# Normalised features split into rounded part and remainder before their transposition instead of after it

## The reference

```python
h = jnp.maximum(_layernorm(x), 0.0); x = x + chebyshev(h, adj)     # 4 orders, weights (4, 64, 64)
h = jnp.maximum(_layernorm(x), 0.0); x = x + attention(h, adj)     # encoder 64->128, 2 layers, 3-layer MLP
h = jnp.maximum(_layernorm(x), 0.0); x = x + gcn(h, adj)
h = jnp.maximum(_layernorm(x), 0.0); x = x + step_layer(h, adj)    # t = adj @ h; 1 where t > 0.5
```

## Time and profile before

| | |
|---|---|
| time, median of 3 runs | 767.3 us (766.12 to 768.61) |
| profiled execution, own time | 764.17 us |
| its span, first to last instruction | 762.3 us |
| busy: PE / DVE / ACT / POOL | 714.2 / 587.6 / 441.8 / 337.7 us |
| granted TensorE clock, mean share of full | 0.991 |
| L881 (split behind the transposition) | 32 x 0.69 us |
| L867 (duplicating copy) | 32 x 0.29 us (median) |

### The profile page before, as it was taken

One profiled execution on the slowest core, in us unless ns is written; L12 is line 12 of the kernel. 1 busy time (PEld: TensorE's weight loads), 2 busy tenths in 40 slices (PEclk: granted clock), 3 DMA queues, 4 the chain that ended last, 5 costly groups with the idle time before them and its releaser, 6 DMA issues.

```text
span 762.3 us, 11361 instructions
## 1 busy us (share of the span) xinstructions
PE 714.2 (94%) x3615; PEld 510.0 (67%) x3615; DVE 587.6 (77%) x1719; ACT 441.8 (58%) x933; POOL 337.7 (44%) x457
## 2 busy tenths in 40 slices
PE   8787999999999999999999999999999999989886
PEld 5365767667676767667676767767676767665663
DVE  3565688889797988889797988889797888676533
ACT  3264658564756757574756757574765747627430
POOL 4343427263553726364553726364453815422301
PEclk9999999999999999999999999999999999999999
DMA  6100100302012030202012030302012030100000
GB/s 180 63 1 0 63 15 1 88 10 84 15 33 66 8 91 1 84 15 84 14 31 68 8 91 0 84 15 84 14 26 73 8 91 6 30 1 21 1 8 7
DMA packets 37386, 30.14 MB, mean 40 GB/s; under 512 B 24016, under 2 KB 25552, under 8 KB 37328
## 3 DMA queue, kind: packets, MB, share of 16 engines
q1 hardware_dynamic: 36336, 29.20, 13.9%
q10 hardware_dynamic: 992, 0.23, 0.1%
HBM read 27.27 MB, written 2.15 MB: 39 GB/s over the span
## 4 chain that ended last, share of the span: by engine, by line
PE 70%; ACT 14%; DVE 8%; issue 4%; POOL 3%; POOLq 0%; DVEq 0%; ACTq 0%
PE turn_ps L1319 13%; PE pre_ps L1162 9%; PE post_ps L1162 7%; PE turn_ps L1285 4%; ACT negz L768 3%; PE score_ps L1270 3%; PE score_ps L1267 3%; PE score_ps L1271 3%; ACT pt L775 3%; PE qkv_ps L1249 3%; PE pre_ps L1121 3%; PE pre_ps L1178 2%; ACT z_t L789 2%; PE post_ps L1328 2%; PE pre_ps L1150 2%
## 5 line engine op out<-in xcount | busy, mean ns | idle before, releaser
L1319 PE MATMUL turn_ps<-pt,v_n 128*128 128x512 f32 x224 | 102.2, 599 | 11.0 <-ACT pt L775 11.0
L768 ACT ACTIVATE negz<-negz,negmax 128x512 f32<-128x512 f32 x128 | 91.7, 718 | 26.9 <-DVE negmax L977 26.6
L969 DVE TENSOR_TENSOR score_ps<-score_ps,a_nat 128x512 f32<-128x512 f32 x128 | 88.9, 695 | 7.9 <-PE score_ps L1271 7.3
L977 DVE CUSTOM_DVE_ANT_0 negz<-score_ps,gate 128x512 f32<-128x512 f32 x128 | 88.5, 691 | 4.5 <-POOL gate L637 0.2
L1162 PE MATMUL pre_ps<-at_hi,u_pair_pre 128*128 128x512 f32 x192 | 85.9, 447 | 4.7 <-DVE u_pair_pre L887 4.1
L566 POOL TENSOR_TENSOR rstd_post<-vareps_post,nhalf 128x4 f32<-128x4 f32 x32 | 32.7, 1020 | 115.0 <-DVE vareps_post L849 114.0
L716 ACT ACTIVATE y_t_pre<-pre_ps 128x512 f32<-128x512 f32 x48 | 28.5, 593 | 93.2 <-PE pre_ps L1162 91.8
L775 ACT ACTIVATE pt<-turn_ps 128x512 f32<-128x512 f32 x128 | 73.8, 591 | 10.3 <-PE turn_ps L1285 10.3
L1319 PEld LDWEIGHTS turn_ps<-pt,v_n 128*128 128x128 f32 x224 | 40.5, 190 | 55.1 <-issue 40.2
L1162 PE MATMUL pre_ps<-at_lo,u_pair_pre 128*128 128x512 f32 x192 | 76.5, 398 | 0.0
L1285 PE MATMUL turn_ps<-ident,negz 128*128 128x128 f32 x512 | 73.4, 275 | 0.2 <-ACT pt L775 0.2
(11 more groups left out here) (169 smaller groups left out, 1764.2 us busy)
## 6 DMA issues: line engine op xcount, KB each, us to landing
a_nat<-in_adj SPq DMA_DIRECT2D x15, 1024.0 KB, 5.6
inv_row<-inv_d SPq DMA_DIRECT2D x28, 256.0 KB, 3.5
x_in<-in_x SPq DMA_DIRECT2D x16, 128.0 KB, 2.2
out<-x_out SPq DMA_DIRECT2D x16, 128.0 KB, 2.5
a_nat<-in_adj SPq DMA_DIRECT2D x4, 256.0 KB, 4.6
inv_d<-inv_total SPq DMA_DIRECT2D x28, 2.0 KB, 2.2
cheb_ws<-in_L_gnn_weight ACTq DMA_DIRECT2D x2, 64.0 KB, 3.2
att_w<-in_L_gnn_a_wv SPq DMA_DIRECT2D x2, 64.0 KB, 3.9
```

The costliest lines, as they stand in the source:

```text
L768: sc.activation(probs[:, i, :], negz[:, i, :], ACT.Exp, bias=negmax[:, i:i + 1], scale=-1.0, accum_out=total[:, i:i + 1]).then_inc(probs_d ...
L969: ve.tensor_tensor(score_ps[i % 2][:], score_ps[i % 2][:], a_nat[s][:, i, :], ALU.mult)\
L977: ve.tensor_tensor_reduce(negz[:, i, :], score_ps[i % 2][:], gate[:, i, :], -1.0, 3.0e38, ALU.add, ALU.min, negmax[:, i:i + 1]).then_inc(b ...
L1319: mm = te.matmul(turn_ps[0][:], v_n[a][:, j * P:(j + 1) * P], pt[:, j, :], start=(j == 0), stop=(j == RB - 1))
```

## The change

VectorE makes the pair before the transposition. `norm_apply` writes `h` to `h_nat`, casts it with rounding to `h_pair[:, :, 0, :]`, waits, and subtracts to get `h_pair[:, :, 1, :]`; only then is `h_ready` counted. TensorE transposes `h_pair`, ScalarE copies the bank to `h_t` as before, and that copy is already rounded part above and remainder below. `split_ht` and its semaphore go, and `cheb_weights` and `encode` wait for ScalarE's copy. All other entries of the lists keep their order.

```diff
@@ ORDER["vector"]; likewise in HEAD and TAIL: every "cheb_ht-n" and "enc_ht-n" of vector goes
-        stats_cheb-0 enc_ht-1 norm_cheb-0 gcn_fold-3 stats_last-3 split_at0-0 split_at1-0
-        mask0.2-2 split_at2-0 norm_last-3 mask1.2-2 split_at3-0 cheb_ht-0 mask2.2-2
+        stats_cheb-0 norm_cheb-0 gcn_fold-3 stats_last-3 split_at0-0 split_at1-0 mask0.2-2
+        split_at2-0 norm_last-3 mask1.2-2 split_at3-0 mask2.2-2
...
@@ tiles and semaphores
-        h_nat = {"pre": sb("h_nat_pre", [P, RB, 2, C]), "post": sb("h_nat_post", [P, RB, C])}
+        h_nat = {t: sb(f"h_nat_{t}", [P, RB, C]) for t in ("pre", "post")}
+        h_pair = sb("h_pair", [P, RB, 2, C], F32R)
...
-        ht_split = sem("ht_split")
...
-        dve_pre = Chain(sem("dve_pre"), 2 * 6 + 10)
+        dve_pre = Chain(sem("dve_pre"), 2 * 7 + 10)
...
@@ norm_apply
-                to = h_nat[t][:, :, 0, :] if t == "pre" else h_nat[t][:]
-                one = ve.scalar_tensor_tensor(to, centred[t][:], 0.0, over_blocks(rstd[t][:]),
+                to = h_nat[t]
+                one = ve.scalar_tensor_tensor(to[:], centred[t][:], 0.0, over_blocks(rstd[t][:]),
                                               ALU.max, ALU.mult)
...
                 chain.add(one)
                 dve.wait_ge(chain.sem, chain.so_far())
-                ve.tensor_copy(h_nat[t][:, :, 1, :], to).then_inc(h_ready[t], 1)
+                chain.add(ve.tensor_copy(h_pair[:, :, 0, :], to[:]))
+                dve.wait_ge(chain.sem, chain.so_far())
+                ve.tensor_tensor(h_pair[:, :, 1, :], to[:], h_pair[:, :, 0, :].bitcast(F32), ALU.subtract)\
+                    .then_inc(h_ready[t], 1)
...
-            def split_ht(g, k):
-
-                dve.wait_ge(ht_copied, 2 * g.n + k + 1)
-                ve.tensor_tensor(h_t[C:P, :], ht_bank(g, k)[C:P, :], h_t[C:P, :].bitcast(F32),
-                                 ALU.subtract).then_inc(ht_split, 1)
...
@@ turn_h, cheb_weights and encode of TensorE
-                                      h_nat["pre"][:, i, :, :].rearrange("p a c -> p (a c)"), ident[:])
+                                      h_pair[:, i, :, :].rearrange("p a c -> p (a c)").bitcast(F32), ident[:])
...
-                pe.wait_ge(ht_split, 2 * g.n + 1)
+                pe.wait_ge(ht_copied, 2 * g.n + 1)
...
-                pe.wait_ge(ht_split, 2 * g.n + 2)
+                pe.wait_ge(ht_copied, 2 * g.n + 2)
```

More of the change, by code:

```diff
@@ L58 @@
         invert.1-2 stats_gcn-3 cheb_fold1-1 stats_enc-1 norm_gcn-3 attend.1-2 norm_enc-1
-        stats_cheb-0 enc_ht-1 norm_cheb-0 gcn_fold-3 stats_last-3 split_at0-0 split_at1-0
-        mask0.2-2 split_at2-0 norm_last-3 mask1.2-2 split_at3-0 cheb_ht-0 mask2.2-2
-        cheb_weights-0 mask3.2-2 last_fold-3 invert.2-2 cheb_fold3-0 mask0.1-1 mask1.1-1
-        attend.2-2 mask2.1-1 cheb_fold2-0 mask3.1-1 mlp3-2""".split(),
+        stats_cheb-0 norm_cheb-0 gcn_fold-3 stats_last-3 split_at0-0 split_at1-0 mask0.2-2
+        split_at2-0 norm_last-3 mask1.2-2 split_at3-0 mask2.2-2 cheb_weights-0 mask3.2-2
+        last_fold-3 invert.2-2 cheb_fold3-0 mask0.1-1 mask1.1-1 attend.2-2 mask2.1-1
+        cheb_fold2-0 mask3.1-1 mlp3-2""".split(),
     "gpsimd": """
@@ L93 @@
     "vector": """
[L94 to L101, removed]
+        stats_cheb-0 norm_cheb-0 split_at0-0 split_at1-0 split_at2-0 cheb_weights-0 split_at3-0
+        cheb_fold3-0 cheb_fold2-0 cheb_fold1-0 stats_enc-0 norm_enc-0 stats_cheb-1 split_at0-1
+        norm_cheb-1 split_at1-1 split_at2-1 split_at3-1 mask0.1-0 mask1.1-0 cheb_weights-1
+        mask2.1-0 mask3.1-0 invert.1-0 cheb_fold3-1 attend.1-0 cheb_fold2-1 cheb_fold1-1
+        stats_enc-1 mask0.2-0 norm_enc-1 mask1.2-0 mask2.2-0 stats_cheb-2 split_at0-2
+        norm_cheb-2 split_at1-2 mask3.2-0 split_at2-2 split_at3-2 invert.2-0 cheb_weights-2
+        mask0.1-1 mask1.1-1 attend.2-0 cheb_fold3-2 mask2.1-1 cheb_fold2-2 mask3.1-1 mlp3-0""".split(),
     "gpsimd": """
@@ L141 @@
         invert.1-2 stats_gcn-3 cheb_fold1-1 norm_gcn-3 stats_enc-1 attend.1-2 norm_enc-1
-        stats_cheb-0 gcn_fold-3 enc_ht-1 stats_last-3 mask0.2-2 mask1.2-2 norm_last-3 mask2.2-2
+        stats_cheb-0 gcn_fold-3 stats_last-3 mask0.2-2 mask1.2-2 norm_last-3 mask2.2-2
         split_at0-0 mask3.2-2 split_at1-0 last_fold-3 invert.2-2 mask0.1-1 norm_cheb-0
[L144 to L151, removed]
+        split_at2-0 mask1.1-1 attend.2-2 mask2.1-1 split_at3-0 mask3.1-1 cheb_weights-0 mlp3-2
+        invert.1-1 stats_gcn-2 norm_gcn-2 attend.1-1 cheb_fold3-0 gcn_fold-2 cheb_fold2-0
+        stats_last-2 mask0.2-1 norm_last-2 cheb_fold1-0 stats_enc-0 mask1.2-1 norm_enc-0
+        mask2.2-1 mask3.2-1 last_fold-2 invert.2-1 attend.2-1 mask0.1-0 mask1.1-0 mask2.1-0
+        mask3.1-0 invert.1-0 mlp3-1 stats_gcn-1 attend.1-0 norm_gcn-1 mask0.2-0 gcn_fold-1
+        stats_last-1 mask1.2-0 norm_last-1 mask2.2-0 mask3.2-0 invert.2-0 last_fold-1 attend.2-0
+        mlp3-0 stats_gcn-0 norm_gcn-0 gcn_fold-0 stats_last-0 norm_last-0 last_fold-0""".split(),
     "gpsimd": """
@@ L170, with __init__ @@
 class Chain:
-    def __init__(self, sem, per_graph):
-        self.sem, self.per, self.made = sem, per_graph, {}
+    def __init__(self, sem, per_graph, since=0):
+        self.sem, self.per, self.made, self.since = sem, per_graph, {}, since
     def turn_to(self, g):
@@ L184, in so_far @@
     def so_far(self):
-        return self.per * self.n + self.made.get(self.n, 0)
+        return self.per * (self.n - self.since) + self.made.get(self.n, 0)
 def graph_layers(nc, x, adj, cheb_w, cheb_b, enc_w, enc_b, att_w, att_b, w1, b1, w2, b2, w3, b3,
@@ L1056, in _ @@
                 "split_at1": split_at(1), "split_at2": split_at(2), "split_at3": split_at(3),
-                "cheb_ht": lambda g: split_ht(g, 0),
                 "cheb_weights": cheb_weights, "cheb_fold3": cheb_fold3,
@@ L1060, in _ @@
                 "stats_enc": stats_enc, "norm_enc": enc_norm,
-                "enc_ht": lambda g: split_ht(g, 1),
                 **layer(0, mask0=mask(0), mask1=mask(1), mask2=mask(2),
```

## The result

| | before | after |
|---|---|---|
| time, median | 767.3 us (766.12 to 768.61, 4 runs) | 779.67 us (777.79 to 780.2, 4 runs) |
| profiled execution, own time | 764.17 us | 777.79 us |
| its span | 762.3 us | 775.9 us |

The ratio is 1.016 with a 95% interval of 1.0125 to 1.0194. The forecast was 779.0 us.

A forecast was written before the change was run, and what follows sets the result against it. TensorE was taken to bound a good round. Nine good rounds (+14.9), three lost (+0.8) and head and tail (-1.2) gave +14.5 on 764.2: 778.7, taken as 779.0 us with the offset to the median; range 769 to 785.

The forecast's parts named there:

- second conflict: `gcn_fold`'s second VectorE instruction meets GpSimd's `k_lo`; forecast to begin at 378.68 and end at 379.73, after `k_lo`'s 379.45.
- Part 1: VectorE's instructions: busy time falls by 8.6 us before contention, gaining nothing by itself in a round bound by TensorE.
- Part 2: `norm_enc` to `encode`: the transposes start 0.2 us late, and `q_lo` and `k_lo` move by the same 0.2 us.
- Part 3: `stats_cheb` and `norm_cheb`: 0.47 us later, so the cast loses to `q_lo`; `stats_last` begins 8.69 us after `attend.1`.
- races: Whether `norm_cheb`'s copy or cast, or GpSimd's `q_lo`, gets the port first; all twelve forecast lost, chance 0.72.
- The sum: Round of 44.35 us: nine good rounds +14.9, three lost +0.8, head and tail -1.2; +14.5 on 764.2 gives 778.7 us.
- lost round of before: Round of the kernel before where `q_lo` delays `norm_cheb`'s copy: 44.10 us against 42.69 for a good one; three of twelve.
- Head and tail: Outside the twelve rounds: L1218 waits of 2.2 us go, L867 waits grow by 0.46 each; -1.2 us (-2.2 to +0.5).
- The offset to the median: Median 3.1 us above the profiled execution, read as about two more lost races; most not added, 779.0 us taken.
- The relief: Rival: VectorE, freed of L881, finishes `norm_cheb` before `q_lo` arrives in every round; 760 us, chance 0.07.
- VectorE keeping the port: Rival: VectorE holds the port over `norm_cheb`'s cast and subtraction, `q_lo` starting at 377.3; 770.6 us, chance 0.12.
- The subtraction meeting `k_lo` as well: Rival: `norm_cheb`'s subtraction also waits for `k_lo`, `stats_last` 0.65 us later still; 787 us, chance 0.05.

The follow-up runs named there:

- e1: Changed kernel with GpSimd's second-layer `q_lo` and `k_lo` cut to 8 of 512 columns from the second graph on: 760.88 us, ratio 0.9992 to the kernel before.
- e2: Changed kernel with second-layer `q_lo` made to wait, in the twelve steady rounds, until `norm_cheb`'s pair is done: 771.42 us, ratio 1.0136 to the kernel before.
- e4: Changed kernel with `gcn_fold`'s intermediate result kept in PSUM: 770.58 us, ratio 1.0119 to the kernel before.
- e5: Kernel before, changed only for `norm_enc` and `encode`; the pair for `cheb_weights` still made behind the transposition: 781.04 us, ratio 1.0172.
- e6: Kernel before, changed only for `norm_cheb` and `cheb_weights`; `encode`'s pair stays the old way: 774.66 us, ratio 1.0083.
- e9: Kernel before, unedited, run again for its spread: median 764.5 us over 12 runs (760.93 to 768.92), 7 of 12 rounds lost in the profiled run.
- e10: Kernel before with `q_lo` waiting for `norm_cheb`'s copy, repeating e3 on another chip: 758.65 us, ratio 0.9924, no rounds lost.
- e3: Kernel before with `q_lo` made to wait until `norm_cheb`'s copy is done: 760.73 us, ratio 0.9992.
- e11: Kernel before with `gcn_fold`'s intermediate result kept in PSUM and no wait for `q_lo`: 761.61 us, ratio 0.9959.
- e8: Kernel before with both edits, `q_lo` waiting for `norm_cheb`'s copy and `gcn_fold`'s intermediate in PSUM: 758.42 us, ratio 0.9888.
- e7: Changed kernel with both edits, `q_lo` waiting for the pair and `gcn_fold`'s intermediate in PSUM: 767.19 us, ratio 0.9998 to the kernel before.

## Why the prediction was right, and where it was off

The mechanism was right and is shown: e1 takes GpSimd's instructions away and the loss with them, e2 turns the order of arrival and makes the cast short again, e4 prices the second conflict.

**Part 1** held. VectorE's 8.6 us of removed work bought nothing; its busy time rose by 0.9.

**Part 2** held within hundredths: `q_lo` was put at +5.23 and came at +5.26 or so, `k_lo` at +7.02 and came at +7.05. It took 1.32 us where 1.37 was named: L857 held it up for 0.05 and not 0.1 us.

**Part 3** held: the cast was to begin at +5.50 and end at +6.76 and did so from +5.49 to +6.73; `stats_last` was put at +8.69 and began at +8.64. L1021 ends 0.28 us behind `k_lo` in both; `k_lo` was put at +7.02 to +8.37, 0.08 us longer than its bare 1.27 and without a reason given, and ran from +7.05 to +8.32. The margin, put at 0.26 us, is 0.23, and all twelve rounds lose; so they do in e5, where it is nearly the same, while in e6, where it is next to nothing, the races fall both ways.

**The sum.** A round was put at 44.35 and takes 44.23 to 44.30 (eleven) and 44.86 (one): 15.0 us for the twelve against 15.7. Eleven of them are 0.14 us above a lost round of before (44.12), though `stats_last` moved by 0.23: neither that nor Part 2's 0.2 us shows in full in a round. TensorE's waits for `at_lo` are 12.8 us, twelve times, not 14.

**Head and tail** were put at -1.2 and came out at -1.4, but by other terms. The waits for the pair (now L1123) grew as foreseen, from 5.6 us in the two places of the head to 6.5. The step that failed is the gain at L1218 in the tail. These two waits of 1.7 us did go (only 0.2 is left, at the first matmul of `encode`), and the tail is still 0.3 us longer. The waits of TensorE in the tail, before:

```profile
PE pre_ps L1218 <- DVE h_t L881: 1.7, 2, 1.0
PE post_ps L1162 <- DVE u_pair_post L887: 1.6, 2, 0.8
PE post_ps L1178 <- ACT y_t_post L716: 0.9, 2, 0.7
```

and after:

```profile
PE post_ps L1155 <- DVE u_pair_post L882: 2.1, 3, 0.8
...
PE post_ps L1171 <- ACT y_t_post L714: 1.5, 3, 0.7
...
PE post_ps L1321 <- DVE h_t L990: 0.5, 1, 0.5
PE pre_ps L1211 <- ACT h_t L708: 0.2, 1, 0.2
```

1.7 us of one wait turned into 0.5, 0.6, 0.5 and 0.2 of others: the `norm_enc` chain was not the only one that was late there, and a wait that goes is worth only what the next one leaves. The head gained 1.7 us instead. Of these, 0.75 stand already at the first transpositions of `h` (9.05 against 9.80 us) and come from the clock: by the trace it is at full from 6.5 us on in this execution and from 8.0 in that of before, and a 128x128 transposition of `a_nat` takes 0.27 us at 7.10 here and still 0.42 at 7.69 there. That is not the change's doing: this moment lies between 6.25 and 8.08 us in the profiles of the kernels with the old pair and between 5.05 and 7.92 in those with the new one. The chain from the first `norm_enc` to `encode` gave 0.27, as predicted; the rest of the head's gain is not traced. That -1.4 and -1.2 agree is chance.

**The offset to the median.** I expected that the 3.1 us between the profiled execution and the median would mostly not come on top, since no race is open any more. The changed kernel's four runs lie within 2.4 us, but its profiled execution is the lowest of them, 1.9 us below the median, where 0.3 had been allowed. So the nearness of 779.0 to 779.67 is in part luck: the profiled execution came 0.9 us below the 778.7 of the sum, and the offset 1.6 us above its term. The four runs are too few to say what the offset is made of. e9 supports the reading for the kernel before: its spread of 8 us comes with a number of lost races that differs from one execution to the next.

**The rivals.** The relief (760 us) needed `q_lo` 0.45 us later; it came 0.03 later. VectorE keeping the port (770.6) is refuted by e6's 1.38 us subtraction. The subtraction meeting `k_lo` as well (787) did not come: it begins 0.28 us ahead of `k_lo` and takes at most 0.43 us. The forecast and 770.6 us differ by the very step that the earlier trace rows decided. (The upper end of the range, 785, is 779 + 5 = 784 by its own terms.)

## What to carry to other kernels

Before adding a VectorE instruction with two SBUF inputs, or moving a copy or cast, lay GpSimd's instructions of that stretch beside it and compare arrival times; where two arrive within a hundredth of a microsecond, a few nanoseconds decide each round, and a program differs from itself by a per cent. A semaphore that fixes the order (0.8% in e10, nothing measurable in e3) or an operand kept in PSUM (0.4% in e11, 1.1% with both in e8) can then be worth more than the instructions saved, if the engine that is made to wait has the time: on the changed kernel the hold only moved the conflict (e2) or made `k_lo` late (e7). An instruction that stood for the port was recognised here by its end, 0.15 us (copy or cast) or 0.28 us (the subtractions and `gcn_fold`) behind the end of GpSimd's. A freed engine gained nothing where it wasn't the bound, but half a microsecond on it can shift everything behind it past such a meeting.

## What was not expected of the hardware

- An unchanged program lost the same race in 3 of 12 rounds in one execution and 7 of 12 in another, with both starts within 0.01 us in every lost round. Over 48 such rounds of four kernels the outcome followed the recorded order of arrival to the nanosecond: lost with `q_lo` 5 to 8 ns ahead, won with it at most 4 ns ahead.
- Between two dependent VectorE instructions GpSimd gets in even when VectorE won the first: the subtraction of e6 took 1.38 instead of 0.43 us, so a won race was worth nothing there (`stats_last` at +8.44 to +8.53 against +8.41 in the lost rounds).
- The VectorE instruction with one PSUM operand took its bare 0.42 us in each of its 16 executions in e4, twelve of them beside `k_lo`. All of L1021 in e4 (ns, min/median/max), and in the changed kernel:

```profile
L1021 DVE SCALAR_TENSOR_TENSOR x<-post_ps,x x16: 424/425/425, 119.0 to 755.0; 128x256 f32<-128x256 f32 x16
```

```profile
L1021 DVE SCALAR_TENSOR_TENSOR x<-s,x x16: 424/1043/1136, 117.9 to 763.6; 128x256 f32<-128x256 f32 x16
```

- TensorE's granted clock fell to 1.2 GHz for 6.8 us in the heads of e5 and e1 and stayed at 2.4 GHz in the changed kernel and e7, after the same 2.4 us of idle time.
